# A float32 LoRA product and feed-forward on one core: the first unit of weights alone in pieces, the second by halves

## The chip, the cores and the metric

The kernel runs on one core of a Trainium2 chip. The metric is the device time of the program in microseconds, the median of several runs; less is better. One of the executions was also taken by the hardware profiler, and all rows below are from it.

## The reference

For each of 8 batches a weight matrix is picked by an adapter number, the activations are multiplied by it, a permuted, block-diagonal feed-forward with an exact GELU follows, and the result is added to the input:

```
w = weight[adapter_ids]                     # (8, 1024, 1024)
y = einsum('bsi,boi->bso', x, w)            # x: (8, 256, 1024) float32
t = y.reshape(2048, 1024)[:, perm].reshape(2048, 16, 64)
t = gelu(einsum('bhd,hdm->bhm', t, up))     # up: (16, 64, 256)
t = einsum('bhm,hmd->bhd', t, down)         # down: (16, 256, 64)
out = x + t.reshape(2048, 1024)[:, unperm].reshape(8, 256, 1024)
```

## The kernel before, in words

**Units.** The first product is cut into 32 units (`NL`), four for each batch: unit g multiplies all 256 tokens of batch g // 4 by 256 rows of that batch's weights. A unit has 8 k steps of 128 inputs and 2 column blocks of 128 outputs. To keep float32 accuracy, weights and x are each split into a high and a low part of type float32r: ScalarE copies the raw values into the high part (`w_hi`, `x_hi`), VectorE subtracts it from the raw values for the low part (`w_lo`, `x_lo`). For each k step and column block TensorE does one matmul of 512 columns (high weights by the high and low parts of x side by side, `x_pair`) and one of 256 (low weights by the high part of x). VectorE then sums the two halves of the accumulator (`y_sum`, line 518), and ScalarE's queue writes the result to a DRAM tensor (`y_park`, line 396). The feed-forward (up, GELU, down) follows behind with its rows gathered by GpSimd; it begins near 75 us and is woven between later units.

**Loads.** A unit's raw weights are 1 MiB and lie in one of four buffers (`w_raw`, `WRAW`); there are two buffers of high and low parts (`WS`). A batch's x is 1 MiB too, in one raw buffer. SP issues the weight loads in order (`load_w`, line 234), each after the low part of the unit that had the buffer before; behind the fourth unit of a batch stand the next batch's x (line 241) and the read of its adapter number (`adapter_of`, line 219).

**The start.** `FIRST` cuts the 8 k steps of the first loads into four pieces of 1, 2, 2 and 3 k steps (128, 256, 256 and 384 KB). ScalarE's queue issues the first three pieces of x, SP the fourth. Units 0 and 1 (`PAIR`) are both made in these pieces: SP's order is the weights 0.0, 0.1, 1.0, 0.2, x's piece 3, then 1.1, 0.3, 1.2, 1.3 (unit.piece; `load_first_w`, lines 247 and 253), and ScalarE's copies (line 427, x: 422), VectorE's subtractions (line 540, x: 534) and TensorE's pieces (`first_lora_piece`, lines 608 and 613) follow the order 0.0, 0.1, 1.0, 0.2, 1.1, 0.3, 1.2, 1.3. Unit 2 comes by two halves of 512 KB (line 227), and ScalarE's copy of its first half (line 372) waits for unit 0's piece 2 (`first_half_done`), that of its second half for unit 0's end. It is multiplied like all later ones (`lora_unit`, lines 643 and 647), which wait for the high and the low part of each half. Before all that TensorE does eight warming matmuls (line 599).

**Counts.** `w_hi_done` and `w_lo_done` count the halves done from unit 2 on, `lora_done` column blocks of all units. GpSimd's late gathers (line 305) and SP's loads wait on these counts.

Of the kernel before, what the change touches and what calls it, by code (L numbers as in the profile page):

```python
# [7 lines left out]
F32 = mybir.dt.float32  # L8
# [23 lines left out]


FIRST = [(0, 1), (1, 3), (3, 5), (5, KT)]
# [4 lines left out]
X_AHEAD = 2  # L39


HALF_PIECE = 2

# [30 lines left out]
def build(nc, x_cols, x_rows, x_late, w, up, down, perm, ids, out_rows, out_late):  # L74
# [3 lines left out]
    with ctx:  # L78
# [48 lines left out]
        perm_in = sem("perm_in")  # L127
        first_w_in = [[sem(f"first_w_in{g}_{n}") for n in range(PIECES)] for g in range(PAIR)]
        first_x_in = [sem(f"first_x_in{n}") for n in range(PIECES)]
        w_in = [sem(f"w_in{i}") for i in range(WRAW)]  # L130
        third_w_in = [sem(f"third_w_in{n}") for n in range(2)]
        x_in = sem("x_in")
# [10 lines left out]
        ones_set = sem("ones_set")  # L143
        first_w_hi = [sem(f"first_w_hi{g}") for g in range(PAIR)]
        first_w_lo = [sem(f"first_w_lo{g}") for g in range(PAIR)]
        first_x_hi = sem("first_x_hi")
# [7 lines left out]
        up_lo_done = sem("up_lo_done")  # L154
        first_half_done = sem("first_half_done")
        lora_done = sem("lora_done")
# [55 lines left out]
        def w_landed(g):  # L212

            return 16 * (g // WRAW + (g % WRAW > PAIR))

        @block.sync
        def _(sp):
            def adapter_of(b):
                return sp.value_load(ids[0:1, b:b + 1], min_val=0, max_val=NW - 1)  # L219

            def w_rows(adapter, i, k):
                return w[bass.ds(adapter * LPB + i, 1), :, k, :].rearrange("a p k o -> (a p) k o")

            def load_third_w(adapter):
                for n in range(2):
                    k = slice(n * HALF, (n + 1) * HALF)
                    sp.dma_start(w_raw[:, PAIR, k, :], w_rows(adapter, PAIR, k)).then_inc(third_w_in[n], 16)
# [17 lines left out]
            def load_first_w(g, n):  # L245
                k = slice(*FIRST[n])
                sp.dma_start(w_raw[:, g, k, :], w_rows(adapter, g, k)).then_inc(first_w_in[g][n], 16)  # L247

            for n in range(PIECES):
                load_first_w(0, n)  # L250
                if n + 1 >= X_BY_ACT and n + 1 < PIECES:
                    k = slice(*FIRST[n + 1])
                    sp.dma_start(x_raw[:, k, :], x_cols[0, :, k, :]).then_inc(first_x_in[n + 1], 16)
                if n > 0:
                    load_first_w(1, n - 1)
            load_first_w(1, PIECES - 1)
            load_third_w(adapter)
            for g in range(PAIR + 1, NL):
                if g % LPB == 0:
                    adapter = adapter_of(g // LPB)  # L260
                load_w(g, adapter)
                if g % LPB == 3 and g // LPB + 1 < B:
                    load_x(g // LPB + 1)
                if g == UP_AFTER:
                    sp.dma_start(up_raw[:, :, :], up).then_inc(up_in, 16)
                if g == DOWN_AFTER:
                    sp.dma_start(down_sb[:, :, :, :], down).then_inc(down_in, 16)

        @block.gpsimd
        def _(pool):  # L270
# [30 lines left out]
            def gather_late_rows(b):  # L301

                g = NL - WRAW + b // 2
                pool.wait_ge(w_lo_done, 2 * (g - PAIR + 1))
                nc.gpsimd.indirect_dma_start(late_rows[:, b, :], None, x_late, block_rows(b)).then_inc(late_rows_in[b], 16)  # L305
# [57 lines left out]
        def _(act):  # L363
            def third_w_high(n):
                act.wait_ge(third_w_in[n], 16)

                if n == 0:
                    act.wait_ge(first_half_done, 1)
                else:
                    act.wait_ge(lora_done, OT)  # L370
                k = slice(n * HALF, (n + 1) * HALF)
                nc.scalar.activation(w_hi[:, PAIR % WS, k, :], w_raw[:, PAIR, k, :], ACT.Copy).then_inc(w_hi_done, 1)

# [49 lines left out]

            def first_w_high(g, n):
                k = slice(*FIRST[n])
                act.wait_ge(first_w_in[g][n], 16)
                nc.scalar.activation(w_hi[:, g, k, :], w_raw[:, g, k, :], ACT.Copy).then_inc(first_w_hi[g], 1)  # L427

# [12 lines left out]
            for n in range(2):  # L441
                third_w_high(n)
            w_high(PAIR + 1)

# [41 lines left out]
        def _(dve):  # L486
            def w_low_half(g, n):
                k = slice(n * HALF, (n + 1) * HALF)
                dve.wait_ge(w_hi_done, 2 * (g - PAIR) + n + 1)
                nc.vector.tensor_tensor(w_lo[:, g % WS, k, :], w_raw[:, g % WRAW, k, :],  # L490
                                        w_hi[:, g % WS, k, :].bitcast(F32), ALU.subtract).then_inc(w_lo_done, 1)
# [44 lines left out]

            def first_w_low(g, n):
                k = slice(*FIRST[n])
                dve.wait_ge(first_w_hi[g], n + 1)
                nc.vector.tensor_tensor(w_lo[:, g, k, :], w_raw[:, g, k, :], w_hi[:, g, k, :].bitcast(F32),  # L540
                                        ALU.subtract).then_inc(first_w_lo[g], 1)

# [52 lines left out]
        def _(pe):  # L595
# [4 lines left out]

            def first_lora_piece(g, n):
                ks = range(*FIRST[n])
                pe.wait_ge(first_x_lo, n + 1)
                pe.wait_ge(first_w_hi[g], n + 1)
                for o in range(OT):
                    col = slice(o * P, (o + 1) * P)
                    for k in ks:
                        nc.tensor.matmul(y_bank(g, o), w_hi[:, g, k, col], x_pair[:, 0, k, :, :], start=(k == 0), stop=False)  # L608
                pe.wait_ge(first_w_lo[g], n + 1)
                for o in range(OT):  # L610
                    col = slice(o * P, (o + 1) * P)
                    for k in ks:
                        last = nc.tensor.matmul(y_bank(g, o)[:, 0, :], w_lo[:, g, k, col], x_hi[:, 0, k, :], start=False, stop=(k == KT - 1))  # L613
                    if n == PIECES - 1:
                        last.then_inc(lora_done, 1)
                if g == 0 and n == HALF_PIECE:
                    last.then_inc(first_half_done, 1)

            def lora_unit(g):
# [14 lines left out]
                for o in range(OT):  # L634
                    col = slice(o * P, (o + 1) * P)
                    acc = y_bank(g, o)
                    for n in range(2):
                        ks = range(n * HALF, (n + 1) * HALF)

                        if o == 0:  # L640
                            pe.wait_ge(w_hi_done, 2 * (g - PAIR) + n + 1)
                        for k in ks:
                            nc.tensor.matmul(acc, w_hi[:, ws, k, col], x_pair[:, xs, k, :, :], start=(k == 0), stop=False)  # L643
                        if o == 0:
                            pe.wait_ge(w_lo_done, 2 * (g - PAIR) + n + 1)
                        for k in ks:
# [118 lines left out]
```

## Time and profile before

| | us |
|---|---|
| median of 3 runs | 298.36 |
| lowest and highest | 298.32, 301.4 |
| the profiled execution, its own time | 298.39 |
| its span, first to last instruction | 296.5 |
| TensorE busy in the span | 290.6 |

The profiled execution's time has about 1.9 us outside the span. Its granted TensorE clock is 0.998 of full speed on the mean.

### The profile page before, as it was taken

To read this page: it belongs to the slowest core of one execution; us is meant where nothing else is said; L and a number is where in the kernel's file an instruction comes from. 1 tells how busy PE (TensorE), PEld (TensorE's weight loads), DVE (VectorE), ACT (ScalarE), POOL (GpSimd) and SP (SyncE) were. 2 spreads that over 40 slices of the span, in tenths; PEclk is the share of its full clock that TensorE was granted. 3 is DMA by queue.
4 is the path that set the end of the run, shared out by engine and by line. 5 is a ranking of instruction groups with operands and counts; after the bars stand their busy time and mean duration, and the time that the engine had idled before them with its cause. 6 is when DMAs were issued, how large, how long until landed. Compare 5 with 4: busy or idle time off the path is not lost.

```text
span 296.5 us, 4330 instructions
## 1 busy us (share of the span) xinstructions
PE 290.6 (98%) x1680; PEld 212.2 (72%) x1680; DVE 179.6 (61%) x211; ACT 159.7 (54%) x179; POOL 98.1 (33%) x92
## 2 busy tenths in 40 slices
PE   8999999999999999999999999999999999999994
PEld 3788888888888838887488864888568885444441
DVE  2789769689778445963558736585446523343333
ACT  3665354367673368344585265822854207777750
POOL 3000000078653007860527005701473415222234
PEclk9999999999999999999999999999999999999999
DMA  6999999999988946899575983866752854421335
GB/s 182 355 428 419 408 428 420 345 302 384 373 358 268 381 163 182 294 349 407 217 253 180 352 316 111 319 222 209 245 183 88 290 184 117 133 71 71 143 143 212
DMA packets 23699, 77.87 MB, mean 263 GB/s; under 512 B 2688, under 2 KB 11264, under 8 KB 18816
## 3 DMA queue, kind: packets, MB, share of 16 engines
q1 hardware_dynamic: 7056, 43.39, 38.7%
q0 software_dynamic: 7488, 25.18, 25.0%
q10 hardware_dynamic: 9136, 9.05, 8.8%
q8 instruction: 13, 0.21, 0.3%
q14 instruction: 6, 0.05, 0.0%
HBM read 60.82 MB, written 16.78 MB: 262 GB/s over the span
## 4 chain that ended last, share of the span: by engine, by line
PE 95%; DMA 1%; SPq 1%; POOL 1%; issue 0%; DVE 0%; ACT 0%; POOLq 0%; DVEq 0%
PE ps L643 38%; PE ps L647 19%; PE ps L700 19%; PE ps L676 6%; PE ps L679 5%; PE ps L682 5%; PE ps L608 3%; DMA w_raw<-w 1%; PE ps L613 1%; POOL out_late L317 1%; SPq L219 1%; DVE w_raw L528 0%; ACT w_hi L427 0%; SPq L247 0%; POOLq L359 0%
## 5 line engine op out<-in xcount | busy, mean ns | idle before, releaser
L643 PE MATMUL ps<-x_pair,w_hi 128*128 128x512 f32 x480 | 131.3, 395 | 0.0
L379 ACT ACTIVATE w_hi<-w_raw 128x1024 fp32r<-128x1024 f32 x58 | 58.4, 1057 | 63.4 <-PE ps L647 52.5
L413 ACT ACTIVATE hidden<-ps 128x1024 f32<-128x1024 f32 x64 | 61.6, 1029 | 55.4 <-PE ps L682 55.4
L643 PEld LDWEIGHTS ps<-x_pair,w_hi 128*128 128x128 f32 x480 | 82.0, 188 | 12.5 <-issue 1.8
L647 PEld LDWEIGHTS ps<-x_pair,w_lo 128*128 128x128 f32 x480 | 73.5, 188 | 10.4
L490 DVE TENSOR_TENSOR w_lo<-w_raw,w_hi 128x1024 fp32r<-128x1024 f32 x60 | 71.0, 1221 | 11.7 <-ACT w_hi L379 11.1
L647 PE MATMUL ps<-x_pair,w_lo 128*128 128x256 f32 x480 | 76.3, 281 | 0.0
L290 POOL DMA_INDIRECT t_raw<-y_rows,idx x32 | 35.4, 1106 | 115.8 <-DMA y_rows<-y_out 100.1
L518 DVE TENSOR_REDUCE y_out<-ps 128x256 f32<-128x512 f32 x64 | 42.9, 686 | 24.6 <-PE ps L647 24.6
L700 PE MATMUL ps<-hidden,down_sb 128*64 128x512 f32 (+1 forms) x264 | 57.4, 583 | 0.0
L510 DVE TENSOR_TENSOR t_lo<-t_raw,t_hi 128x512 fp32r<-128x512 f32 x32 | 21.7, 694 | 47.8 <-ACT t_hi L403 47.8
L700 PEld LDWEIGHTS ps<-hidden,down_sb 128*64 128x64 f32 x264 | 18.0, 137 | 34.0 <-issue 30.9
L296 POOL DMA_INDIRECT rows<-x_rows,idx x16 | 22.9, 1429 | 14.7 <-PE ps L647 10.7
L676 PE MATMUL ps<-t_hi,up_hi 64*128 64x512 f32 x128 | 26.9, 417 | 0.0
L309 POOL DMA_INDIRECT out_rows<-rows,idx x16 | 19.4, 1211 | 18.2 <-DVE rows L528 14.5
L679 PE MATMUL ps<-t_lo,up_hi 64*128 64x512 f32 x128 | 25.1, 389 | 0.0
L682 PE MATMUL ps<-t_hi,up_lo 64*128 64x512 f32 x128 | 24.9, 386 | 0.0
L403 ACT ACTIVATE t_hi<-t_raw 128x512 fp32r<-128x512 f32 x32 | 19.9, 642 | 0.6 <-DMA t_raw<-y_rows,idx 0.6
L676 PEld LDWEIGHTS ps<-t_hi,up_hi 64*128 64x128 f32 x128 | 12.0, 184 | 11.4 <-issue 7.3
L499 DVE TENSOR_TENSOR x_pair<-x_raw,x_pair 128x2048 fp32r<-128x2048 f32 x7 | 16.1, 2293 | 4.9 <-ACT x_pair L385 4.7
L528 DVE TENSOR_TENSOR rows<-ps,rows 128x512 f32<-128x512 f32 x16 | 11.0, 690 | 10.3 <-PE ps L700 10.3
L305 POOL DMA_INDIRECT w_raw<-x_late,idx x8 | 8.4, 1046 | 23.1 <-DVE w_lo L490 17.0
(29 smaller groups left out, 116.8 us busy)
## 6 DMA issues: line engine op xcount, KB each, us to landing
w_raw<-w SPq DMA_DIRECT2D x29, 1024.0 KB, 7.2
y_rows<-y_out ACTq DMA_DIRECT2D x32, 256.0 KB, 6.8
x_raw<-x_cols SPq DMA_DIRECT2D x7, 1024.0 KB, 9.4
w_raw<-w SPq DMA_DIRECT2D x4, 256.0 KB, 5.5
w_raw<-w SPq DMA_DIRECT2D x2, 512.0 KB, 8.4
hidden<-up SPq DMA_DIRECT2D x1, 1024.0 KB, 11.9
down_sb<-down SPq DMA_DIRECT2D x1, 1024.0 KB, 11.5
w_raw<-w SPq DMA_DIRECT2D x2, 384.0 KB, 7.2
```

Of the source, the lines that this page charges most:

```text
L290: nc.gpsimd.indirect_dma_start(t_raw[:, f % TG, :], None, y_rows[0:D * (chunk + 1), :], rows_of(f)).then_inc(t_in[f % TG], 16)
L296: nc.gpsimd.indirect_dma_start(row_place(f), None, x_rows, rows_of(f)).then_inc(rows_in[f % XR], 16)
L379: nc.scalar.activation(w_hi[:, g % WS, k, :], w_raw[:, g % WRAW, k, :], ACT.Copy).then_inc(w_hi_done, 1)
L413: nc.scalar.activation(hidden[:, f % HS, m, :, :], up_banks(f, m)[:, :, :], ACT.Gelu).then_inc(gelu_done, 1)
L490: nc.vector.tensor_tensor(w_lo[:, g % WS, k, :], w_raw[:, g % WRAW, k, :], w_hi[:, g % WS, k, :].bitcast(F32), ALU.subtract).then_inc(w_lo ...
L518: nc.vector.tensor_reduce(y_out[:, g % YS, o, :], y_bank(g, o).rearrange("p c s -> p s c"), mybir.AxisListType.X, ALU.add).then_inc(y_summ ...
L643: nc.tensor.matmul(acc, w_hi[:, ws, k, col], x_pair[:, xs, k, :, :], start=(k == 0), stop=False)
L647: last = nc.tensor.matmul(acc[:, 0, :], w_lo[:, ws, k, col], x_hi[:, xs, k, :], start=False, stop=(k == KT - 1))
L676: nc.tensor.matmul(acc[:, h, :], up_hi[own, f % FU, col], t_hi[own, ts, :], start=True, stop=False)
L679: nc.tensor.matmul(acc[:, h, :], up_hi[own, f % FU, col], t_lo[own, ts, :], start=False, stop=False)
L682: last = nc.tensor.matmul(acc[:, h, :], up_lo[own, f % FU, col], t_hi[own, ts, :], start=False, stop=True)
L700: last = nc.tensor.matmul(acc[h * DH:(h + 1) * DH, :], down_sb[:, 2 * (f % FU) + h, m, :], hidden[:, f % HS, m, h, tok], start=(m == 0), s ...
```

## The change

Only unit 0 is made in the four pieces. Unit 1 is loaded, copied and subtracted by two halves, as unit 2 was, and multiplied by `lora_unit` behind unit 0; unit 2 stays in halves, and its high copies now wait for unit 0's last column block (`lora_done`) alone. SP's order becomes 0.0, 0.1, 0.2, x's piece 3, 0.3, unit 1's halves, unit 2's halves, unit 3. On VectorE the sum of unit 0's output stands between the low parts of units 1 and 2. The counts of halves now begin with unit 1.

```diff
-HALF_PIECE = 2
+HALVED = (1, 2)
...
             def load_w(g, adapter):
-                if WRAW <= g < WRAW + PAIR:
-                    sp.wait_ge(first_w_lo[g - WRAW], PIECES)
-                elif g >= WRAW + PAIR:
-                    sp.wait_ge(w_lo_done, 2 * (g - WRAW - PAIR + 1))
+                if g == WRAW:
+                    sp.wait_ge(first_w_lo, PIECES)
+                elif g > WRAW:
+                    sp.wait_ge(w_lo_done, 2 * (g - WRAW))
...
             for n in range(PIECES):
-                load_first_w(0, n)
+                load_first_w(n)
                 if n + 1 >= X_BY_ACT and n + 1 < PIECES:
                     k = slice(*FIRST[n + 1])
                     sp.dma_start(x_raw[:, k, :], x_cols[0, :, k, :]).then_inc(first_x_in[n + 1], 16)
-                if n > 0:
-                    load_first_w(1, n - 1)
-            load_first_w(1, PIECES - 1)
-            load_third_w(adapter)
-            for g in range(PAIR + 1, NL):
+            for g in HALVED:
+                for n in range(2):
+                    load_w_half(g, n, adapter)
+            for g in range(HALVED[-1] + 1, NL):
...
-            def third_w_high(n):
-                act.wait_ge(third_w_in[n], 16)
-
-                if n == 0:
-                    act.wait_ge(first_half_done, 1)
-                else:
-                    act.wait_ge(lora_done, OT)
+            def w_high_half(g, n):
+                act.wait_ge(half_w_in[HALVED.index(g)][n], 16)
+                if g >= WS:
+                    act.wait_ge(lora_done, OT * (g - WS + 1))
                 k = slice(n * HALF, (n + 1) * HALF)
-                nc.scalar.activation(w_hi[:, PAIR % WS, k, :], w_raw[:, PAIR, k, :], ACT.Copy).then_inc(w_hi_done, 1)
+                nc.scalar.activation(w_hi[:, g % WS, k, :], w_raw[:, g % WRAW, k, :], ACT.Copy).then_inc(w_hi_done, 1)
...
-                first_w_high(0, n)
-                if n > 0:
-                    first_w_high(1, n - 1)
-            first_w_high(1, PIECES - 1)
-            for n in range(2):
-                third_w_high(n)
-            w_high(PAIR + 1)
+                first_w_high(n)
+            for g in HALVED:
+                for n in range(2):
+                    w_high_half(g, n)
+            w_high(HALVED[-1] + 1)
...
-                first_w_low(0, n)
-                if n > 0:
-                    first_w_low(1, n - 1)
-            first_w_low(1, PIECES - 1)
-            w_low(PAIR)
+                first_w_low(n)
+            w_low(1)
+            y_sum(0)
+            w_low(2)
...
-                        y_sum(g)
+                        if g > 0:
+                            y_sum(g)
...
             for n in range(PIECES):
-                first_lora_piece(0, n)
-                if n > 0:
-                    first_lora_piece(1, n - 1)
-            first_lora_piece(1, PIECES - 1)
+                first_lora_piece(n)
...
-                    if g >= PAIR:
+                    if g > 0:
                         lora_unit(g)
```

## Rows read from the trace of the kernel before

**Rows 1.** The page, parts 1 and 2: busy time, and clock over the span.

```profile
PE 290.6 (98%) x1680; PEld 212.2 (72%) x1680; DVE 179.6 (61%) x211; ACT 159.7 (54%) x179; POOL 98.1 (33%) x92
...
PEclk9999999999999999999999999999999999999999
```

**Rows 2.** Table by stretches: length, busy us, granted clock, DMA share, GB/s.

```profile
6.25:8.10 1.85, 1.45 (x7) 0.69 (x5) 0.54 (x2) 1.00 (x2) 0.14 (x1) 1.00 0.84 173
8.10:11.94 3.84, 3.73 (x20) 3.13 (x21) 2.41 (x5) 2.24 (x5) 0.00 (x0) 1.00 0.99 353
...
19.30:78.40 59.10, 59.10 (x347) 51.23 (x345) 48.80 (x52) 30.51 (x30) 14.91 (x10) 1.00 0.99 385
78.40:242.00 163.60, 163.60 (x956) 123.64 (x955) 100.77 (x115) 86.00 (x94) 63.16 (x54) 1.00 0.75 260
```

**Rows 3.** The chain that ended last, 3 to 21 us: start, length, what.

```profile
3.13 4.16 DMA w_raw<-w
...
7.32 0.64 ACT w_hi L427
...
8.10 1.16 PE ps L608 x4
9.26 0.48 PE ps L613 x4
...
11.84 0.10 issue
11.94 1.16 PE ps L608 x4
...
13.58 1.67 PE ps L608 x6
15.25 0.72 PE ps L613 x6
15.97 0.93 PE ps L608 x4
16.90 0.47 PE ps L613 x4
...
19.46 0.92 PE ps L643 x4
```

**Rows 4.** Three loads of SP: issue (start, length), then KB and us to landing.

```profile
4.19 0.33 SPq L247 DMA_DIRECT2D w_raw<-w  x1
w_raw<-w SPq DMA_DIRECT2D x1, 256.0 KB, 5.0
...
4.56 0.44 SPq L253 DMA_DIRECT2D x_raw<-x_cols  x1
x_raw<-x_cols SPq DMA_DIRECT2D x1, 384.0 KB, 5.9
...
5.71 0.33 SPq L247 DMA_DIRECT2D w_raw<-w  x1
w_raw<-w SPq DMA_DIRECT2D x1, 384.0 KB, 6.6
```

**Rows 5.** Timeline of ScalarE, 11 to 20 us; in brackets its idle time before, releaser.

```profile
11.16 0.63 ACT L427 ACTIVATE w_hi<-w_raw 128x512 fp32r<-128x512 f32 x1 [1.24 <-DMA w_raw<-w]
...
13.64 0.63 ACT L427 ACTIVATE w_hi<-w_raw 128x512 fp32r<-128x512 f32 x1 [0.38 <-DMA w_raw<-w]
14.59 0.85 ACT L427 ACTIVATE w_hi<-w_raw 128x768 fp32r<-128x768 f32 x1 [0.31 <-DMA w_raw<-w]
15.85 1.06 ACT L372 ACTIVATE w_hi<-w_raw 128x1024 fp32r<-128x1024 f32 x1 [0.42 <-DMA w_raw<-w]
...
19.62 1.06 ACT L379 ACTIVATE w_hi<-w_raw 128x1024 fp32r<-128x1024 f32 x1 [1.42 <-DMA w_raw<-w]
```

**Rows 6.** Timeline of VectorE, 9 to 24 us.

```profile
9.43 0.69 DVE L534 TENSOR_TENSOR x_pair<-x_raw,x_pair 128x512 fp32r<-128x512 f32 x1
...
12.56 0.96 DVE L534 TENSOR_TENSOR x_pair<-x_raw,x_pair 128x768 fp32r<-128x768 f32 x1
...
19.38 2.48 DVE L518 TENSOR_REDUCE y_out<-ps 128x256 f32<-128x512 f32 x4
21.77 2.35 DVE L490 TENSOR_TENSOR w_lo<-w_raw,w_hi 128x1024 fp32r<-128x1024 f32 x2
```

More of the change, by code:

```diff
@@ L127, in build @@
         perm_in = sem("perm_in")
-        first_w_in = [[sem(f"first_w_in{g}_{n}") for n in range(PIECES)] for g in range(PAIR)]
+        first_w_in = [sem(f"first_w_in{n}") for n in range(PIECES)]
         first_x_in = [sem(f"first_x_in{n}") for n in range(PIECES)]
         w_in = [sem(f"w_in{i}") for i in range(WRAW)]
-        third_w_in = [sem(f"third_w_in{n}") for n in range(2)]
+        half_w_in = [[sem(f"half_w_in{g}_{n}") for n in range(2)] for g in HALVED]
         x_in = sem("x_in")
@@ L143, in build @@
         ones_set = sem("ones_set")
-        first_w_hi = [sem(f"first_w_hi{g}") for g in range(PAIR)]
-        first_w_lo = [sem(f"first_w_lo{g}") for g in range(PAIR)]
+        first_w_hi = sem("first_w_hi")
+        first_w_lo = sem("first_w_lo")
         first_x_hi = sem("first_x_hi")
@@ L212, in w_landed @@
         def w_landed(g):
-            return 16 * (g // WRAW + (g % WRAW > PAIR))
+            return 16 * (g // WRAW + (g % WRAW > HALVED[-1]))
         @block.sync
@@ L222, in w_rows, with load_w_half @@
                 return w[bass.ds(adapter * LPB + i, 1), :, k, :].rearrange("a p k o -> (a p) k o")
-            def load_third_w(adapter):
-                for n in range(2):
-                    k = slice(n * HALF, (n + 1) * HALF)
-                    sp.dma_start(w_raw[:, PAIR, k, :], w_rows(adapter, PAIR, k)).then_inc(third_w_in[n], 16)
+            def load_w_half(g, n, adapter):
+                k = slice(n * HALF, (n + 1) * HALF)
+                sp.dma_start(w_raw[:, g, k, :], w_rows(adapter, g, k)).then_inc(half_w_in[HALVED.index(g)][n], 16)
             def load_w(g, adapter):
-                if WRAW <= g < WRAW + PAIR:
-                    sp.wait_ge(first_w_lo[g - WRAW], PIECES)
-                elif g >= WRAW + PAIR:
-                    sp.wait_ge(w_lo_done, 2 * (g - WRAW - PAIR + 1))
+                if g == WRAW:
+                    sp.wait_ge(first_w_lo, PIECES)
+                elif g > WRAW:
+                    sp.wait_ge(w_lo_done, 2 * (g - WRAW))
                 sp.dma_start(w_raw[:, g % WRAW, :, :], w_rows(adapter, g % LPB, slice(0, KT))).then_inc(w_in[g % WRAW], 16)
@@ L243, in _, with load_first_w @@
             adapter = adapter_of(0)
-            def load_first_w(g, n):
+            def load_first_w(n):
                 k = slice(*FIRST[n])
-                sp.dma_start(w_raw[:, g, k, :], w_rows(adapter, g, k)).then_inc(first_w_in[g][n], 16)
+                sp.dma_start(w_raw[:, 0, k, :], w_rows(adapter, 0, k)).then_inc(first_w_in[n], 16)
             for n in range(PIECES):
-                load_first_w(0, n)
+                load_first_w(n)
                 if n + 1 >= X_BY_ACT and n + 1 < PIECES:
@@ L422, in first_x_high, with first_w_high @@
                 nc.scalar.activation(x_hi[:, 0, k, :], x_raw[:, k, :], ACT.Copy).then_inc(first_x_hi, 1)
-            def first_w_high(g, n):
+            def first_w_high(n):
                 k = slice(*FIRST[n])
-                act.wait_ge(first_w_in[g][n], 16)
-                nc.scalar.activation(w_hi[:, g, k, :], w_raw[:, g, k, :], ACT.Copy).then_inc(first_w_hi[g], 1)
+                act.wait_ge(first_w_in[n], 16)
+                nc.scalar.activation(w_hi[:, 0, k, :], w_raw[:, 0, k, :], ACT.Copy).then_inc(first_w_hi, 1)
             act.wait_ge(ones_set, 1)
@@ L607, in first_lora_piece @@
                     for k in ks:
-                        nc.tensor.matmul(y_bank(g, o), w_hi[:, g, k, col], x_pair[:, 0, k, :, :], start=(k == 0), stop=False)
-                pe.wait_ge(first_w_lo[g], n + 1)
+                        nc.tensor.matmul(y_bank(0, o), w_hi[:, 0, k, col], x_pair[:, 0, k, :, :], start=(k == 0), stop=False)
+                pe.wait_ge(first_w_lo, n + 1)
                 for o in range(OT):
@@ L612, in first_lora_piece @@
                     for k in ks:
-                        last = nc.tensor.matmul(y_bank(g, o)[:, 0, :], w_lo[:, g, k, col], x_hi[:, 0, k, :], start=False, stop=(k == KT - 1))
+                        last = nc.tensor.matmul(y_bank(0, o)[:, 0, :], w_lo[:, 0, k, col], x_hi[:, 0, k, :], start=False, stop=(k == KT - 1))
                     if n == PIECES - 1:
                         last.then_inc(lora_done, 1)
-                if g == 0 and n == HALF_PIECE:
-                    last.then_inc(first_half_done, 1)
             def lora_unit(g):
```

22 lines of the change are left out of this document (10 added, 12 removed).

## The prediction

> **What bounds the kernel now.** I read the page's first part, then the chain of waits, then a table by stretches, and last the timelines of ScalarE and VectorE over the first 20 us with the landings of the loads. The page gives TensorE 98% of the span at the full granted clock [rows 1], so time can only be won or lost where TensorE waits. The table by stretches says where that is: from 19.30 to 242.00 us TensorE is busy for all of 59.10 and all of 163.60 us, at clock 1.00 [rows 2]. Nothing in that stretch can be shortened or hurt by this change as long as it stays without a wait; it can only be moved as a block. The edits all act before it. So the question is one number: when does the first matmul of unit 2 (line 643) start? On the chain it is 19.46 us [rows 3].
>
> The chain ahead of it: the second weight piece lands at 7.29 (3.13 + 4.16), its high part takes 0.64 us on ScalarE, and TensorE takes over at 8.10 [rows 3]. From there the chain is TensorE alone. What is its work? A k step of one unit, two 512-column and two 256-column matmuls, costs 0.70 us by the undisturbed part of the chain (0.93 + 0.47 for two k steps), so a unit costs 8 x 0.70 = 5.61. At 8.10 one k step of 16 is done, and 15 x 0.70 = 10.53 would end at 18.63. The actual end, 19.46, is 0.83 later: three restarts at 0.23 to 0.27 each (1.16 and 1.67 us where 0.93 and 1.40 are the rule), and a 0.10 wait at 11.84 [rows 3]. That 0.83 us is all the change could win behind 8.10. What it could lose is set by the loads. The kernel before gives TensorE two units of work for each piece of x, and so never runs ahead of the loads by more than 0.1 us.
>
> **The change, part by part.** *Matmuls:* the same number, 0.00. Only the order differs: all of unit 0, then all of unit 1.
>
> *Piece 1 of unit 0:* its load is the second of SP's in both kernels, so TensorE again starts at 8.10, and ends it at 8.10 + 1.16 + 0.48 = 9.73 [rows 3]. There stood unit 1's piece 0 and there stands unit 0's piece 2 now.
>
> *Piece 2 (k 3 and 4):* its weights are issued at 4.19 and land 5.0 later, at 9.2 [rows 4]; now one load of 128 KB less lies ahead. At the 353 GB/s of 8.10 to 11.94 [rows 2] that is 0.37 us, so 8.8. ScalarE needs 0.63 for it (x's part, already there, is done before), which gives 9.5, and 0.14 later TensorE may start: 9.6, just ahead of the 9.73 at which it is free. VectorE's low part of x for this piece is 0.69 us behind ScalarE's (at 8.6), 9.4 [rows 6]. So no wait, and piece 2 ends at 9.73 + 1.40 = 11.13.
>
> *Piece 3 (k 5 to 7):* this step decides. It needs the last pieces of x and of unit 0's weights, 2 MiB landed in all. In the kernel before the load that completes 2 MiB (x in three pieces, unit 0's first three, unit 1's first two, x's last) is unit 1's piece 1, whose high part begins at 11.16 after 1.24 us of waiting for it [rows 5]. The other way round: the weights' last piece is issued at 5.71 and lands 6.6 later, at 12.3 [rows 4]; it now has 384 KB fewer ahead (unit 1's first two pieces), at 353 to 370 GB/s some 1.1 us: 11.2. Both ways agree on 11.15. x's last piece, at 4.56 + 5.9 = 10.46 [rows 4], moves up by the 0.37 of the 128 KB to 10.1; its high part takes 0.84, its low part 0.96 [rows 5, 6], so it is ready at 11.95 and is not last. The weights' high part goes from 11.15 to 12.0 (0.85 for this shape [rows 5]); TensorE starts 0.14 later, at 12.15, after a wait of 1.0 us that the kernel before has not. Both loads are also issued 0.5 and 1.0 us earlier; in the early stretch 6.25 to 8.10 the queues moved only 173 GB/s at 0.84 share [rows 2], so some of it may be issue and not bytes. If the last load came earlier by the whole 1.0 beyond the bytes' 1.1, it would land at 10.2; if the first slow stretch repeats and nothing of the bytes is won back, at 11.6. I take 11.15, by the row with the same 2 MiB, and keep 10.2 and 11.6 as ends. Piece 3 then costs, restart included, 1.67 + 0.72 = 2.39 [rows 3]: 14.55. Its low part is ready at 12.0 + 0.96, needed 1.6 us behind the start: covered.
>
> *Unit 1 by halves:* 3 x 1 MiB and x are the same bytes, so 2.5 MiB are there between unit 0's last piece (2.375 MiB, 12.3) and unit 1's third (2.625 MiB, 13.6): 13.0; and 3 MiB at 14.6, as the wait of 0.31 at 14.59 shows [rows 4, 5]. A half costs ScalarE 1.06 and VectorE 1.2 [rows 5, 6]. First half: high at 14.05, before TensorE is there (14.55); low at 15.3, needed at 14.55 + 0.93 = 15.5. Second half: high 14.6 to 15.65, needed at 15.95; low 15.7 to 16.9, needed at 16.9. The last one has no cover left: I book 0.05, at the least 0, at the most 0.4 (0.15 late and a restart of 0.23). If the wait at piece 3 is shorter than I say, this one grows by as much, since the half's landing does not move with it: the low part at 16.9 leaves 0.47 and the other column block's 2.80 to do, so this half alone holds unit 2 back to 20.2. Two bounds of unlike make give one number. Unit 1 ends, and unit 2 starts, at 14.55 + 5.61 + 0.05 = 20.2.
>
> *Elsewhere:* ScalarE has four copies of unit 1 (2.5 us) replaced by two (2.1), VectorE 2.8 by 2.4; neither is on the path. Unit 2's high copy now waits for unit 0's end (14.55) in place of a half of it; its load lands only at 15.84 [rows 5], which hides that. The reduction of unit 0's output now stands ahead of unit 2's low part on VectorE: 16.9 + 1.25 (two of 0.62 [rows 6]) = 18.15, then low halves to 19.35 and 20.5, needed at 21.1 and 22.5. Cover 1.7 us; without it each us would show. Unit 3's weights land by 19.6 [rows 5] and its high part begins with unit 1's end, 20.2, low halves done by 23.3 and 24.5, needed behind 25.8. SP: the wait for x's low parts before x's next block ends 1.5 us earlier, and so do the adapter read and the load of unit 4 behind it; the load of unit 6 waits for unit 2's low part and goes out at 20.5 instead of 19.64. These only refill a queue that holds 99% from 19.30 to 78.40 while TensorE never waits [rows 2]; cost nothing. GpSimd's waits count the same events under other numbers.
>
> **Sum.** Unit 2 starts at 18.63 (no loss) + 0.23 and 0.27 (restarts at pieces 1 and 3) + 1.02 (the wait at piece 3) + 0.05 (unit 1's second half) = 20.2, where it was 19.46 with 0.83 of loss: +0.74. The block behind it moves whole. The profiled execution took 298.39 us round a span of 296.5, and the median of the runs is 298.36, the same. 298.39 + 0.7 = **299.1 us**.
>
> The Trainium skill speaks against this. "DMA: Bandwidth & Descriptors", section "Anatomy of one DMA", prices a transfer at some 2.0 us fixed and the bytes at 436 GB/s; for 2 MiB from the first issue at about 0.75 us an estimate by that page is 7.6 us. By that, or anything near, the sum would have no wait at piece 3. The trace does not agree: 2 MiB are there at 11.15, and the first stretch ran at 173 GB/s.
>
> **Rivals.**
> *The loads come earlier (no slower, or a little faster).* Mechanism: with unit 1's small pieces out of the queue and both last pieces issued earlier, the slow stretch is cured. For: the queues move 173 GB/s from 6.25 to 8.10 and 353 in the stretch after [rows 2]; at 353 those 1.85 us would bring 0.33 MB more, 0.9 us of every landing behind. Against: the small x and weight pieces ahead of that stretch stay as they are, and x's last piece follows as before. The weights' last piece would land at 10.25, unit 0 end at 13.65, unit 1's second half land at 13.7 with its low part at 16.0, and unit 2 start at 19.3: -0.15, 298.2 us. It decides at two landings, 10.45 for unit 0's last weights (10.45 + 0.85 + 0.14 + 2.39 + 5.61 = 19.45) and 13.85 for unit 1's second half; both must be under. The whole 0.6 (8.10 + 0.23 + 10.53 = 18.86, 297.8 us) would need 10.1 and 13.2.
> *Only piece 3 comes earlier.* Then unit 1's second half is the bound, as worked out above, and the time is the same 299.1 by another wait; were that half 0.4 earlier, 298.7.
> *Both halves late.* Landings of the halves half a us later than the same bytes before: unit 2 at 20.9, 299.8 us.
> *The clock falls in the new wait.* TensorE keeps 1.00 over 6.25 to 8.10 with 1.45 of 1.85 us busy [rows 2]. If 1.0 us of idleness sent it to 1.2 GHz, the 7.7 us of matmuls to unit 2's start would take up to 7.7 more: 307. ("TensorE: Matmul & The Clock Gate", section "What's actually happening", in the Trainium skill has idleness lead to the half clock.)
> *The change does nothing:* unit 0 alone but bound as before, 298.4.
>
> **How the numbers follow.** Small loss of 0.3 to 1.1 us, 0.60; no change within 0.3, 0.19; faster by over 0.3, 0.09; larger loss, 0.10; the clock, 0.02. The likeliest case's own range is 298.7 to 299.5. For 8 in 10 I go to 298.0 and 300.1, which hold the ends 10.2 and 11.6 of the landing, the late halves and most of the early-loads case. A measurement of this kernel can tell about 1%, 3 us, from no change; only the clock case or a disturbance of the whole stream gives that: slower 0.03, faster 0.01, same 0.96.
>
> **What would show it.** Right: a TensorE wait of about 1 us near 11.1 to 12.2, released by ScalarE's copy of the 768-column piece; unit 2's first matmul at 20.2; TensorE unbroken from there for 222 us. Wrong: unit 0's last weight piece landing before 10.5; a wait inside unit 1 longer than 0.4; any TensorE wait behind unit 2; a granted clock under 1.00 in the first 20 us.

## The result and the profile after

Over 22 executions each, the changed kernel takes 299.81 us (299.0 to 301.81) and the one before 298.5 us (297.89 to 301.4): the ratio is 1.0045, with a 95% interval of 1.0034 to 1.0057. That is slower by 1.3 us: a small loss that is clear of the noise, within the 1% (3 us) that the prediction calls no change, and within its range of 298.0 to 300.1. The forecast was +0.7, so the direction and the place of the wait held, and the forecast was about half of what came. The profiled execution, at 300.54 us with a span of 298.8, is one of the slower ones; its own loss is 2.15 us.

The page after, parts 1, 2 and 4:

```profile
PE 291.0 (97%) x1680; PEld 212.6 (71%) x1680; DVE 179.3 (60%) x209; ACT 159.4 (53%) x177; POOL 101.4 (34%) x92
...
PEclk9999999999999999999999999999999999999999
...
PE 94%; DMA 3%; SPq 1%; POOL 1%; issue 1%; ACT 0%; DVE 0%; POOLq 0%; DVEq 0%
```

TensorE's busy time and clock are those of [rows 1]; what has grown is the DMA share of the chain, 1% to 3%. The chain of the changed kernel over its first 22 us shows where (start, length, what); it answers to [rows 3]:

```profile
4.64 7.92 DMA w_raw<-w
12.56 0.02 issue
12.58 0.85 ACT w_hi L418
13.44 0.14 issue
13.57 1.63 PE ps L597 x6
15.20 0.71 PE ps L602 x6
15.91 0.93 PE ps L630 x4
...
21.52 0.93 PE ps L630 x4
```

The second line's end, 12.56, is the landing of unit 0's last weights. It was issued at 4.64, a microsecond earlier than in [rows 4], with 384 KB less ahead of it, and lands 7.92 later instead of 6.6, so 0.25 us later than before. Behind it stand the copy, the 0.14 handover and piece 3 as forecast. Unit 2 starts at 21.52, where it was 19.46: 2.06 of the profiled 2.15 us.

TensorE's timeline after, 9 to 16 us (in brackets the idle time before, and its releaser):

```profile
9.88 1.09 PE L597 MATMUL ps<-x_pair,w_hi 128*128 128x512 f32 x4
10.80 0.63 PE L602 MATMUL ps<-x_pair,w_lo 128*128 128x256 f32 x4
13.57 1.63 PE L597 MATMUL ps<-x_pair,w_hi 128*128 128x512 f32 x6 [2.13 <-ACT w_hi L418]
```

In this window there is one wait, of 2.13 us, at the foreseen place and released by the foreseen copy. ScalarE's timeline after gives the landings, as in [rows 5]:

```profile
11.59 0.84 ACT L413 ACTIVATE x_pair<-x_raw 128x768 fp32r<-128x768 f32 x1 [2.29 <-DMA x_raw<-x_cols]
12.58 0.84 ACT L418 ACTIVATE w_hi<-w_raw 128x768 fp32r<-128x768 f32 x1 [0.15 <-DMA w_raw<-w]
13.83 1.06 ACT L363 ACTIVATE w_hi<-w_raw 128x1024 fp32r<-128x1024 f32 x1 [0.40 <-DMA w_raw<-w]
15.10 1.06 ACT L363 ACTIVATE w_hi<-w_raw 128x1024 fp32r<-128x1024 f32 x1 [0.21 <-DMA w_raw<-w]
```

Read the end of each bracketed wait as a landing: x's last piece at 11.6 (10.46 before), unit 0's last weights at 12.6, unit 1's halves at 13.8 and 15.1. The table by stretches says that it was not for want of bytes. Before, then after, from 5 to 12 us (last number: GB/s):

```profile
5.00:9.00 4.00, 3.60 (x13) 2.09 (x12) 1.90 (x4) 1.73 (x5) 1.17 (x4) 1.00 0.84 236
9.00:12.00 3.00, 2.90 (x19) 2.42 (x17) 1.80 (x4) 1.76 (x4) 0.00 (x0) 1.00 1.04 367
```

```profile
5.00:9.00 4.00, 3.77 (x12) 2.15 (x11) 1.82 (x4) 1.85 (x5) 1.39 (x4) 1.00 0.85 239
9.00:12.00 3.00, 2.44 (x15) 1.97 (x13) 1.19 (x2) 0.71 (x2) 0.00 (x0) 1.00 1.00 365
...
78.40:242.00 163.60, 163.60 (x961) 123.24 (x958) 101.29 (x116) 87.91 (x96) 67.61 (x55) 1.00 0.75 261
```

236 and 239, 367 and 365: the same stream, in which the loads' ends lie elsewhere. And TensorE is again busy without a gap behind the start.

The landing of the weights is not the whole of the wait. x's last piece was forecast for 10.1 and came at 11.59. ScalarE copies it ahead of the weights, and VectorE makes its low part behind that copy:

```profile
12.46 0.96 DVE L523 TENSOR_TENSOR x_pair<-x_raw,x_pair 128x768 fp32r<-128x768 f32 x1 [2.28 <-ACT x_pair L413]
```

It ends at 13.42, where 11.95 was forecast, and 0.04 later TensorE could have used it: x's piece alone would have held TensorE to 13.46, and the weights held it to 13.57. In the second profile of the changed kernel (below) the two are 12.66 and 12.85.

### The profile page after: what moved, and what is told of

Its sections match the earlier page's. It is cut to its first block, busy times and chain, and to the rows that moved or that the text cites. A ratio compares the mean times of both kernels' runs of the same rounds, so it can differ in the third digit from the quotient of the medians.

```text
span 298.8 us, 4316 instructions
## 1 busy us (share of the span) xinstructions
PE 291.0 (97%) x1680; PEld 212.6 (71%) x1680; DVE 179.3 (60%) x209; ACT 159.4 (53%) x177; POOL 101.4 (34%) x92
## 3 DMA queue, kind: packets, MB, share of 16 engines
q10 hardware_dynamic: 9136, 9.05, 8.7%
## 4 chain that ended last, share of the span: by engine, by line
PE 94%; DMA 3%; SPq 1%; POOL 1%; issue 1%; ACT 0%; DVE 0%; POOLq 0%; DVEq 0%
PE ps L630 39%; PE ps L634 20%; PE ps L687 18%; PE ps L663 6%; PE ps L666 5%; PE ps L669 5%; DMA w_raw<-w 3%; POOL out_late L311 1%; PE ps L597 1%; SPq L215 0%; SPq L242 0%; ACT w_hi L418 0%; PE ps L602 0%; DVE w_raw L517 0%; SPq L248 0%
## 5 line engine op out<-in xcount | busy, mean ns | idle before, releaser
L630 PE MATMUL ps<-x_pair,w_hi 128*128 128x512 f32 x496 | 135.9, 395 | 0.0
L630 PEld LDWEIGHTS ps<-x_pair,w_hi 128*128 128x128 f32 x496 | 84.7, 189 | 13.1 <-issue 1.8
L634 PEld LDWEIGHTS ps<-x_pair,w_lo 128*128 128x128 f32 x496 | 76.1, 189 | 10.6
L479 DVE TENSOR_TENSOR w_lo<-w_raw,w_hi 128x1024 fp32r<-128x1024 f32 x62 | 73.4, 1221 | 12.2 <-ACT w_hi L370 11.6
L634 PE MATMUL ps<-x_pair,w_lo 128*128 128x256 f32 x496 | 78.8, 281 | 0.0
L303 POOL DMA_INDIRECT out_rows<-rows,idx x16 | 22.1, 1383 | 18.2 <-DVE rows L517 14.8
L663 PEld LDWEIGHTS ps<-t_hi,up_hi 64*128 64x128 f32 x128 | 12.0, 184 | 11.4 <-issue 7.3
L299 POOL DMA_INDIRECT w_raw<-x_late,idx x8 | 8.3, 1043 | 20.8 <-DVE w_lo L479 14.7
```

The lines of the kernel that those rows point to most:

```text
L634: last = nc.tensor.matmul(acc[:, 0, :], w_lo[:, ws, k, col], x_hi[:, xs, k, :], start=False, stop=(k == KT - 1))
L663: nc.tensor.matmul(acc[:, h, :], up_hi[own, f % FU, col], t_hi[own, ts, :], start=True, stop=False)
```

## The experiments

Each kernel was profiled once (the changed one twice) and timed beside the kernel before. The block behind the start moves whole, so one number of each profile explains its time: the start of unit 2, read from the chain.

| kernel | unit 2 starts | time of that execution | difference | median |
|---|---|---|---|---|
| before | 19.46 | 298.39 | 278.9 | 298.5 |
| changed | 21.52 | 300.54 | 279.0 | 299.81 |
| changed, again | 20.80 | 299.86 | 279.1 | 300.12 |
| halves held for the last weights | 21.39 | 300.45 | 279.1 | 300.59 |
| halves held for piece 1 | 20.63 | 299.62 | 279.0 | 299.47 |
| halves held for piece 0 | 20.83 | 299.72 | 278.9 | 299.74 |
| unit 0 in five pieces | 20.91 | 299.98 | 279.1 | 300.01 |
| x's last piece by ScalarE | 19.21 | 298.32 | 279.1 | 298.85 |
| the same, issued later | 19.89 | 298.86 | 279.0 | 299.76 |
| x's last piece behind the weights | 22.85 | 301.88 | 279.0 | 302.15 |
| unit 1's halves in two transfers each | 21.51 | 300.54 | 279.0 | 299.85 |
| kernel before, only TensorE's order changed | 23.55 | 302.91 | 279.4 | 300.53 |
| kernel before, x's last piece by ScalarE | 19.78 | 299.06 | 279.3 | 298.41 |
| kernel before, unit 1's first piece ahead | 18.95 | 298.33 | 279.4 | 298.55 |

The starts differ by 4.6 us and the differences by 0.5 (0.2 among the versions of the changed kernel). The medians come from four series, in which the kernel before itself took 298.25 to 298.5; the ratios given below compare within a series. By this table, the changed kernel's median of 299.81 stands for a start near 20.8, and the profiled start is 0.7 later than the usual one.

The same rule gives an estimate of the landings that were not profiled. In both profiles of the changed kernel unit 2 starts 8.96 us behind the landing of unit 0's last weights (21.52 - 12.56 and 20.80 - 11.83, to 0.01). Eight of the 22 executions took 299.0 to 299.31 us; 279.0 and 8.96 taken off, that is a landing at 11.0 to 11.35, about where the prediction had it. The median stands for 11.85, and the profile's 12.56 is near the late end. A landing in one profile is therefore one draw from a spread of some 1.5 us, and differences smaller than that between two profiles show little.

**Unit 1's halves held back until unit 0's last weights have landed.**

```diff
+            sp.wait_ge(first_w_in[PIECES - 1], 16)
             for g in HALVED:
```

> The changed kernel, but SP issues unit 1's halves only when unit 0's last weight piece has landed. Theory A (the last piece lands when the slowest of the DMA engines has got through its share, whatever is queued behind): it still lands at 12.0 to 12.6 us. Theory B (the engines that are ahead take unit 1's 4 KB packets and these take memory bandwidth from the ones that lag): it lands by 10.5 to 11.2. Under both the stream has a hole of some 2 us behind it, so the halves land late and the time is 1.5 to 3 us above the changed kernel; the landing is what counts here, not the time.

Its chain:

```profile
4.72 5.26 DMA w_raw<-w
...
10.15 3.80 DMA w_raw<-w
13.95 0.02 issue
13.97 1.06 ACT w_hi L364
```

The same load, issued 0.08 later than in the changed kernel, lands 5.26 later instead of 7.92: at 9.98. So theory A falls: what is queued behind costs unit 0's last weights 2.6 us in this pair of profiles, and 1.9 against the other profile of the changed kernel. x's last piece comes at 9.05 instead of 11.59. A lucky draw is unlikely. The time of this version hangs on that landing, and three of its four executions took 300.45 to 300.69 (the fourth, 302.13, has a clock of 0.993).

What was moved meanwhile, in the changed kernel and then in this one: to 9.98 us, and for this one also from 5 to 9 us:

```profile
0.00:9.98 9.98, 8.29 (x21) 4.55 (x22) 3.71 (x7) 4.51 (x8) 2.56 (x10) 1.00 0.69 210
```

```profile
0.00:9.98 9.98, 8.06 (x23) 4.65 (x24) 3.96 (x8) 5.36 (x9) 2.57 (x10) 1.00 0.62 211
5.00:9.00 4.00, 3.54 (x14) 2.14 (x13) 2.30 (x4) 2.13 (x5) 1.40 (x4) 1.00 0.84 305
```

By 9.98 both have moved 2.10 MB, which is x and unit 0 (2 MiB). In the held kernel it is those and next to nothing else; in the changed kernel some of it belongs to unit 1. The packets in the two traces show the overtaking (on SP's queue those of x's and unit 0's last pieces have 3 KB, those of the halves 4 KB). In the changed kernel the first 4 KB packet starts at 9.22, when 99 of the 256 packets of 3 KB are still to end; the last of these ends at 12.23, and by then 203 packets of unit 1 are through. From 11.5 on the 3 KB packets come one at a time, while the queue moves unit 1 beside them. In the held kernel the last 3 KB packet ends at 9.65. A second thing differs and is not explained: from 5 to 9 us, ahead of unit 1's first packet, the held kernel's stream already ran at 305 GB/s where the changed one's ran at 239.

The price of the hold is the hole that follows (the next load is issued at 10.15), and 300.59 us at the median, ratio 1.0094 (1.0066 to 1.0122).

**The order of TensorE's work alone.** All loads and copies of the kernel before, eight pieces interleaved, only the multiplications one unit after the other:

```diff
-            for n in range(PIECES):
-                first_lora_piece(0, n)
-                if n > 0:
-                    first_lora_piece(1, n - 1)
-            first_lora_piece(1, PIECES - 1)
+            for g in range(PAIR):
+                for n in range(PIECES):
+                    first_lora_piece(g, n)
```

> The kernel before with its loads, copies and subtractions as they were (eight pieces, interleaved), only TensorE takes all four pieces of unit 0 and then those of unit 1. Theory A: unit 0's last piece is ready at 13.4 as in the kernel before, TensorE waits 2.1 to 2.4 us ahead of it and unit 2 starts near 21.6, as in the profiled execution of the changed kernel: 300.3 to 300.8 us, so the order of TensorE's work is the whole loss and the shorter queue brought nothing. Theory C (the shorter queue does bring the 1.1 us that the prediction gave it, and the profiled execution was a bad draw): this one is 1 us slower than the changed kernel's median of 299.8, that is 300.8 or more.

300.53 us at the median of 5, ratio 1.0065 (1.0048 to 1.0082): inside theory A's marks, though its interval overlaps that of the changed kernel. TensorE waits for 2.11 us up to 14.04, 0.6 later than said, and what comes last is x's low part on VectorE. So the reordering of TensorE's work by itself costs about what the change costs. By the ratios, 1.0065 and 1.0045, the shorter queue brought 0.6 us of the 1.1 it was credited with; by their intervals that could be nothing or the whole. The profiled execution, at 302.91, has one thing more, told below under the clock.

**Unit 0 in five pieces, the last of one k step.**

```diff
-FIRST = [(0, 1), (1, 3), (3, 5), (5, KT)]
+FIRST = [(0, 1), (1, 3), (3, 5), (5, 7), (7, KT)]
```

> The changed kernel with unit 0 and its x in five pieces, the last of one k step. Theory A: the last weights still land at 12.0 to 12.6, but only 0.70 us of matmuls stand behind them instead of 2.1, so unit 0 ends at 14.1 to 14.4 instead of 15.9; unit 1's second half then is the bound by its low part on VectorE (17.4) and unit 2 starts at 20.7 to 21.0: 0.6 to 0.9 us faster than the changed kernel, 299.0 to 299.3. If unit 1's second half is no bound, 1.4 us faster: 298.4.

ScalarE's timeline and then the chain:

```profile
12.34 0.42 ACT L418 ACTIVATE w_hi<-w_raw 128x256 fp32r<-128x256 f32 x1 [0.68 <-DMA w_raw<-w]
13.59 1.06 ACT L363 ACTIVATE w_hi<-w_raw 128x1024 fp32r<-128x1024 f32 x1 [0.84 <-DMA w_raw<-w]
```

```profile
13.59 1.07 ACT w_hi L363
14.66 0.02 issue
14.68 1.24 DVE w_lo L479
15.92 0.04 issue
15.96 0.73 PE ps L634 x4
```

The last piece lands at 12.3 and unit 0 is through early, but now the chain goes by unit 1's first half and its low part on VectorE, and unit 2 starts at 20.91, inside the 20.7 to 21.0 of theory A. The median, 300.01 (ratio 1.0056, 1.0040 to 1.0073), is no better than the changed kernel's: my 299.0 to 299.3 was counted from the slow profiled execution, which was a mistake. What it shows is the second bound: finer pieces of unit 0 win nothing, since unit 1's halves stand right behind. (With one load more for x and one for the weights ahead of them, SP also issues the halves 1.2 us later, the first at 6.40.)

**The changed kernel again.** No edit.

> The changed kernel once more, to see how much its first loads differ between executions. Theory B (unit 1's halves, queued right behind, take bandwidth from the engines that lag with unit 0's pieces): unit 0's last weights land at 11.5 to 12.8 us again, long after 2 MiB in all are through, and unit 2 starts at 20.8 to 21.6; median 299.4 to 300.2. Theory L (the profiled execution was a bad draw and the held one of the first series a good one): the landing may come out near 10.5, with unit 2 at 20.2 or earlier.

300.12 us (4 runs, 299.63 to 301.9), ratio 1.0077 (1.0047 to 1.0108), overlapping with the first series' 1.0045. The last weights land at 11.83 (issued at 4.67, 7.16 later), unit 2 starts at 20.80, and x's last piece lands at 10.79, 0.8 earlier than in the first profile. Theory B's marks held and L's did not; but the landing itself differs by 0.7 us between two executions.

**Halves held until piece 1 has landed, and until piece 0 has.** The same line as above with `first_w_in[1]` and `first_w_in[0]`.

> The changed kernel, but SP issues unit 1's halves only when unit 0's weight piece 1 has landed (7.2 to 7.7 us) instead of at 5.2. Theory B: unit 0's last weights land at 10.0 to 10.8 and TensorE's wait ahead of piece 3 is under 0.8 us; the halves' first bytes come at 9.5, behind unit 0's, so no hole: halves land near 12.5 and 13.8, unit 2 starts at 19.4 to 20.0, and the time is 298.3 to 298.9, some 1 us under the changed kernel. Theory A or L (what is queued behind does not matter): last piece at 11.5 to 12.6 as in the changed kernel, halves 0.5 to 1 us later than there, time equal or up to 1 us above.

> The changed kernel, SP issuing unit 1's halves when unit 0's piece 0 has landed (5.5 to 6.7 us) instead of at 5.2. If the loads queued behind slow unit 0's last pieces in proportion to how long they stand in the queue, the weights' last piece lands between the changed kernel's 11.8 to 12.6 and the 10.3 of the version held till piece 1: near 11. If they only need to be there at all, 11.8 to 12.6. In both the time is 299.2 to 300.0.

ScalarE's timeline of the first of the two:

```profile
9.43 0.85 ACT L414 ACTIVATE x_pair<-x_raw 128x768 fp32r<-128x768 f32 x1
10.35 0.85 ACT L419 ACTIVATE w_hi<-w_raw 128x768 fp32r<-128x768 f32 x1
12.91 1.06 ACT L364 ACTIVATE w_hi<-w_raw 128x1024 fp32r<-128x1024 f32 x1 [1.71 <-DMA w_raw<-w]
14.71 1.06 ACT L364 ACTIVATE w_hi<-w_raw 128x1024 fp32r<-128x1024 f32 x1 [0.74 <-DMA w_raw<-w]
```

Held to 7.93, the last weights are there by 10.35 (no wait stands before their copy), and TensorE is busy for all of 9 to 12 us: the wait at piece 3 is gone. Yet unit 2 starts at 20.63, because the second half lands at 14.7 and its low part ends at 17.04; the median is 299.47, ratio 1.0041 (1.0026 to 1.0057), not the 298.3 to 298.9 expected. Landing right, time wrong: the halves came 0.4 and 0.9 us later than I had put them. Held to 6.00 only, the last weights land at 11.9 and the median is 299.74 (1.0041, 1.0020 to 1.0061), as without a hold: the "near 11" of the proportional theory did not come, in one profile.

**Unit 1's halves each in two transfers of 256 KB**, in the same place of the queue.

```diff
+                parts = 2 if g == 1 else 1
+                for part in range(parts):
+                    k = slice(n * HALF + part * HALF // parts, n * HALF + (part + 1) * HALF // parts)
```

> The changed kernel with unit 1's two halves each loaded as two transfers of 256 KB (2 KB per partition instead of 4 KB), in the same place of SP's queue. In the first loads of the kernel before the pieces behind were of 256 and 384 KB, and a load landed 0.4 MiB of the stream behind its place in it; in the changed kernel, with 512 KB halves behind, unit 0's last weights land 0.8 to 0.9 MiB behind. Theory G (what is queued behind matters by its size: the engines that are ahead take long packets, and the others fall back): the last weights land at 10.9 to 11.4 us, the time is 0.4 to 0.8 us under the changed kernel, 299.1 to 299.5. Theory H (only that something is queued behind matters, and how the slowest engine fares): 11.7 to 12.6 as in the changed kernel, 299.7 to 300.1; two transfers more on SP cost nothing.

The last weights land at 11.9, the second half's at 15.6, which is then the bound; 299.85 us, ratio 1.0053 (1.0026 to 1.0080). Landing and median are those of theory H. G's earlier landing did not come, so nothing speaks for the size of what is queued behind; with one profile and a spread of 298.43 to 302.03 it is not excluded.

**x's last piece issued by ScalarE's queue**, in the changed kernel and in the one before; then later, meant for the time at which SP had issued it; then by SP, but behind unit 0's last weights.

```diff
-X_BY_ACT = 3
+X_BY_ACT = 4
```

> The changed kernel with x's last piece issued by ScalarE's queue right behind the third one (at 2.1 us instead of 4.0) and the weights' last piece by SP at 4.1 instead of 4.6. Theory A: the bytes are the same and the slowest engine sets the landing: the weights' last piece lands at 12.0 to 12.6, x's last before 10, weights' pieces 1 and 2 some 0.5 us later; time within 0.5 us of the changed kernel. Theory D (landings hang on issue times and on SP's one queue): the last weights land 0.5 us or more earlier and the time falls by as much.

> The kernel before with x's last piece issued by ScalarE's queue. It separates what that edit does from what unit 0 alone does. If the edit speeds the first stream as a whole (350 to 400 GB/s from 5 to 9 us, as in the changed kernel with the same edit): the kernel before has only 0.83 us of restarts and a 0.1 wait to lose and its start at piece 1 may come 0.3 later, so 298.0 to 298.7, no difference that shows; unit 0 alone with the same edit is then still 0.2 to 0.5 us slower than this or equal. If x's bytes at that place only delay the weights' piece 1: 298.6 to 298.9.

> The changed kernel with x's last piece on ScalarE's queue, but issued as late as SP issued it (4.0 us, behind ScalarE's first copy) instead of at 2.1. Theory E (the queue counts: behind the weights on SP's queue its packets run alone on one queue, on ScalarE's they run beside them): the stream keeps 330 to 400 GB/s from 6 to 9 us, the last weights land by 10.5 and the time is 298.7 to 299.1, as with the early issue. Theory F (the issue time counts): the stream is as slow as in the changed kernel (210 to 270 GB/s) and the last weights land at 11.5 to 12.6; time 299.6 to 300.1.

> The changed kernel with SP issuing unit 0's last weights before x's last piece, both on its queue. Theory E: the stream stays slow and now x's last piece is the late one, landing at 11.8 to 12.6; time as the changed kernel or 0.2 us above, as x's low part is made behind it: 299.7 to 300.3. If x's load at that place were the cause of the slow stretch, the last weights land by 10.5 (x's last piece then by 11.5) and the time falls to 299.3 or less.

The stretches of the changed kernel with this edit, and its chain:

```profile
5.00:9.00 4.00, 3.42 (x11) 1.75 (x10) 1.76 (x4) 1.92 (x5) 1.21 (x5) 1.00 1.02 374
9.00:12.00 3.00, 3.00 (x18) 2.63 (x17) 2.98 (x5) 2.82 (x4) 0.00 (x0) 1.00 1.04 387
```

```profile
8.46 1.17 PE ps L597 x4
9.63 0.47 PE ps L602 x4
10.10 0.92 PE ps L597 x4
11.02 0.47 PE ps L602 x4
11.49 1.39 PE ps L597 x6
12.88 0.71 PE ps L602 x6
13.60 0.93 PE ps L630 x4
```

374 GB/s where there were 239, and from 8.46 the chain is TensorE without a wait or a restart: unit 0 alone can be fed, if the stream is fast. It takes 298.85 us, ratio 1.0017 (1.0008 to 1.0027). In the profiled execution, one of the fastest of the ten, nothing is lost: the first start comes at 8.46 instead of 8.10, the restarts are saved, and unit 2 starts at 19.21. Where the median's 0.5 us go was not profiled. The kernel before with the same edit takes 298.41 us (1.0004, 0.9993 to 1.0014), its stream of 5 to 9 us rising from 236 to 349 GB/s: even when fed, unit 0 alone shows no gain over the pair. Theory D's time held (0.8 us less than the changed kernel by the ratios, 1.0 by the medians), A's did not.

The later issue on ScalarE's queue did not go out at 4.0 us as planned but at 3.1, between the early one's 2.1 and SP's 4.0. The median of ten is 299.76 (1.0044, 1.0026 to 1.0062), that of the changed kernel, with a spread of 298.86 to 301.1. The one profiled execution, the fastest of the ten, looks like E: the last weights land by 10.7, unit 2 starts at 19.89 and the time is 298.86. By the medians F holds: the other queue, even with 0.9 us of earlier issue, brought nothing, and the gain came only with the issue at 2.1. Since the issue time was not the same as SP's, the queue itself stays untested. With the weights' last piece ahead on SP, x's last lands at 11.4 and the median is 302.15 (1.0108, 1.0076 to 1.0141), 2 us more than expected. Most of that is the clock: the two executions at a clock of 1.00 took 299.57 and 300.49.

**The first piece of unit 1 ahead of unit 0's piece 1**, in the kernel before: an attempt to fill the wait ahead of 8.10.

> The kernel before with unit 1's first piece (128 KB) loaded, copied and multiplied ahead of unit 0's piece 1 (256 KB): TensorE gets its second k step of work at 7.5 to 7.9 instead of 8.10. If the weight pieces land in order of their bytes, unit 1's piece 0 lands by 6.9 and up to 0.5 us of the early wait is filled: 297.8 to 298.1. If the second load's landing is set by latency and not by bytes (7.3 for either), nothing: 298.3, or 0.3 worse as piece 1 of unit 0 comes later.

298.55 us, ratio 1.0012 (0.9993 to 1.0032): nothing. In its profile unit 1's piece is there at 7.1 and unit 0's piece 1 at 8.15 instead of 7.29; behind that TensorE runs without the two later restarts, and unit 2 starts at 18.95, 0.5 earlier than in the profile of the kernel before. The time is the same, because what stands behind the start took 279.4 instead of 278.9 us in it; why is open. No version beat the kernel before.

## Why the prediction was right, and where it was short

*The bound.* Right: everything behind unit 2's start moved as a block, TensorE without a wait from 21.52 to 244 us; the table of starts and times shows it for fourteen profiles, to 0.5 us. ScalarE's, VectorE's and SP's later work cost nothing, the moved reduction of unit 0 included: VectorE ended unit 2's low part at 20.89, before TensorE asked for it.

*The start and piece 2.* TensorE took over at 8.40 instead of 8.10 and was free at 11.4 instead of 11.13. In this execution that is hidden in the wait.

*The step that failed* is the landing of the loads that piece 3 needs, and so the term "the wait at piece 3". Unit 0's last weights were taken at 11.15 with ends at 10.2 and 11.6. They came at 12.56 in one profile and 11.83 in the other, and 11.9 in two near relatives, all past the late end; by the estimate from the times, some nine of the 22 executions lie within the ends and the others behind. x's last piece, put at 10.1 and "not last", came at 11.59 and 10.79. By itself it would have held TensorE to within 0.11 and 0.19 us of where the weights did. Only in the version held for piece 0, where it landed at 9.81, are the weights (11.89) alone in being late. Both of my ways to it counted bytes ahead: from the load that completed 2 MiB before, and from 384 KB less in the queue. The bytes were right, for the stream ran at 239 and 365 GB/s as before; what I took over unseen was that a load lands when its place in the stream has passed. The held version shows that 2 MiB with nothing behind land at 9.98; with unit 1's halves behind from 5.2 or 6.0 us, and x's piece on SP's queue, they landed at 11.8 to 12.6 in the profiles. (With x's piece on ScalarE's queue they were there by 10.0 and 10.7 although the halves stood behind.) So much of what the shorter queue ahead should have given went to the loads that moved up behind. That these overtake is shown by the packets: those of unit 1 run for 3 us beside unit 0's last ones. That it is single ones of the 16 engines that lag fits the packets that come one at a time at the end; the traces do not name the engine, so that part is argued, not shown. Why the stream of 5 to 9 us was faster in the held kernels (305 and 313 GB/s) than in the changed one (239 and 260) is open.

*The sum.* The wait at piece 3 was put at 1.02. It was 2.13 in the first profile and 1.27 in the second, whose start of 20.80 is the usual one. The piece with its restart took 2.34 (2.39 forecast) and unit 1 5.61 (5.61), with none of the 0.05 to 0.4 allowed for its second half, since the late start covered it. 18.63 + 0.30 (later first start) + 0.47 (two restarts) + 2.13 (wait) = 21.5. At the usual 20.8 the shift is 1.3 us, which is what was measured. That the range held is owed to its width as well as to the reasoning: 299.1 us itself came in about a third of the executions.

*The rivals.* "Only piece 3 comes earlier" was the best of them. Both the version held for piece 1 and the five pieces took the first bound away and ran into unit 1's halves (the second half in the one, the first in the other), at 20.63 and 20.91, where 20.2 was forecast from the landing at 14.6; the second half's landing at 14.69 was followed by unit 2 after 5.94 us, where 5.6 was forecast; 0.27 of that is a restart. "The loads come earlier" came true only with x on ScalarE's queue, where the profiled start of 19.21 is the rival's 19.3. The estimate of 7.6 us for 2 MiB from the Trainium skill ("DMA: Bandwidth & Descriptors", section "Anatomy of one DMA") is not met by any run: 9.98 is the least seen with x's piece on SP, and with it on ScalarE's queue the last copy began at 10.01 without a wait. The page fits its 2.0 us and 436 GB/s to single transfers issued by GpSimd, and these are eight loads issued by SP and ScalarE.

*The clock* was given 0.02. Its mean is 0.994 in 2 of the 22 executions of the changed kernel, which take 301.71 and 301.81, the two slowest. Of the four executions of the second series one has it too (301.9). So it is about one execution in ten, at 2 us and not at the 7.7 that I had as its price. Without them the median would be 0.1 us lower.

## What to carry to other kernels

Where loads are queued behind one another, bytes ahead of a load give only the earliest time at which it can land; take its landing from a trace in which the same amount of work stands behind it, or hold that work back in an experiment, and look at more than one execution: here the same load's landing moved by 0.7 us between two. Where an engine copies several operands in a fixed order, a late operand ahead of the one you watch sets its time just as well. A pair of units that share their first operand gives TensorE twice the work for each piece landed, and this buffer against late pieces was worth more than the restarts that interleaving cost. When a wait is removed at the start, compute at once where the next load in line binds: here two bounds of the same size stood one behind the other.

## What was unexpected of the hardware

A wait of TensorE of about 2 us in these first microseconds is sometimes followed by half the clock. The kernel with x's last piece behind the weights, TensorE's timeline and then its stretches:

```profile
10.76 0.63 PE L601 MATMUL ps<-x_pair,w_lo 128*128 128x256 f32 x4
13.32 2.56 PE L596 MATMUL ps<-x_pair,w_hi 128*128 128x512 f32 x6 [1.93 <-DVE x_pair L522]
```

```profile
13.30:17.20 3.90, 3.88 (x13) 3.34 (x14) 3.75 (x5) 1.72 (x2) 0.00 (x0) 0.56 1.05 437
17.20:22.80 5.60, 5.60 (x33) 4.89 (x33) 3.65 (x5) 2.01 (x2) 0.00 (x0) 1.00 1.02 410
```

After 1.93 us without work the six high matmuls take 2.56 us where 1.63 is the rule with its restart; the clock, still 1.00 during the wait, is 0.50 from 14.30 to 16.30, which is the lower of its two levels (1.2 and 2.4 GHz), and back at 1.00 behind 17.2. With 0.74 from 13.30 to 14.30 it fell some 0.5 us after TensorE had begun again. The piece costs 3.84 us by the chain instead of 2.34. Six of this kernel's eight executions have the mean clock of 0.994, and it is why its median is 302.15. In the changed kernel's profile a longer wait, 2.13 us, left the clock at 1.00. The version with only TensorE's order changed shows the fall too, in its profiled execution: 2.63 us for the six matmuls behind a wait of 2.11, a mean clock of 0.994, and 302.91 us beside a median of 300.53. So the length of the wait does not decide it alone. "TensorE: Matmul & The Clock Gate" in the Trainium skill, section "What's actually happening", has idleness lead to the half clock; these rows agree in kind. The other surprise is in the experiments: x's last piece issued 1.9 us earlier, on another queue, raised the whole stream of 5 to 9 us from 239 to 374 GB/s in the changed kernel and from 236 to 349 in the one before.
